# Turning attention probabilities with transposing DMAs instead of TensorE, in a mixture-of-experts and attention kernel

## The reference

```python
x = x + 0.5 * ffn(layernorm(x))      # 8 experts, 256 -> 512 -> 256, top-p weights, p = 0.9
x = x + attn(layernorm(x))
x = x + 0.5 * ffn(layernorm(x))

# attn: 16 query heads, 4 key/value heads of 16, rms norm and rotary on q and k
s = einsum('bhqd,bhkd->bhqk', q * scale, k)
s = where(causal, s, -inf)
p = softmax(s, axis=-1)              # 256 x 256 per head
out = einsum('bhqk,bhkd->bqhd', p, v) @ Wo.T + bo
```

## Time and profile before

| | |
|---|---|
| median of 3 runs | 1284.58 us (1283.86 to 1286.27) |
| profiled execution | 1287.02 us, its span 1285.2 us |
| TensorE matmul busy | 1203.9 us, 94% of the span |
| VectorE, ScalarE, GpSimd busy | 909.6, 574.2 and 543.9 us |
| mean granted TensorE clock | 0.989 of full |
| attention stages n = 12 to 27 | about 350 to 1030 us |

### The profile page before, as it was taken

One profiled execution on the slowest core, in us unless ns is written; L12 is line 12 of the kernel. 1 busy time (PEld: TensorE's weight loads), 2 busy tenths in 40 slices (PEclk: granted clock), 3 DMA queues, 4 the chain that ended last, 5 costly groups with the idle time before them and its releaser, 6 DMA issues.

```text
span 1285.2 us, 26968 instructions
## 1 busy us (share of the span) xinstructions
PE 1203.9 (94%) x8096; PEld 743.2 (58%) x8096; DVE 909.6 (71%) x1946; ACT 574.2 (45%) x1086; POOL 543.9 (42%) x659
## 2 busy tenths in 40 slices
PE   3777779999999999999999999999999999999999
PEld 2334435666566666655666666566665666665665
DVE  5767666567788887887788778878876755554444
ACT  2343343333364645554545454545554433333332
POOL 3324225355555455544554555445333333332332
PEclk9899989999999999999999999999999999999999
DMA  5122110000000000000000000000000000000000
GB/s 196 49 68 76 53 49 2 1 2 1 1 1 1 2 2 2 0 0 0 0 0 0 0 0 0 0 1 6 5 6 1 5 5 5 5 5 5 4 4 21
DMA packets 10048, 18.62 MB, mean 14 GB/s; under 512 B 2177, under 2 KB 6785, under 8 KB 9985
## 3 DMA queue, kind: packets, MB, share of 16 engines
q1 hardware_dynamic: 9840, 17.79, 4.1%
q10 hardware_dynamic: 144, 0.01, 0.0%
HBM read 15.70 MB, written 2.10 MB: 14 GB/s over the span
## 4 chain that ended last, share of the span: by engine, by line
PE 53%; issue 17%; DVE 15%; ACT 6%; POOL 5%; DVEq 2%; DMA 1%; ACTq 0%; POOLq 0%
PE U L212 15%; PE G L212 15%; PE YB L238 12%; PE BC L238 4%; ACT room L486 3%; POOL HS L882 2%; DVE X L584 2%; ACT TS L443 2%; DVE MX L713 2%; DVE TS L558 1%; DVE MXW L640 1%; DVE PR L619 1%; PE BB L381 1%; PE BC L357 1%; DVE NB L718 1%
## 5 line engine op out<-in xcount | busy, mean ns | idle before, releaser
L882 POOL TENSOR_TENSOR HS<-H,HS 128x512 f16<-128x512 f32 x256 | 299.0, 1169 | 469.8 <-ACT HS L450 420.7
L212 PE MATMUL G<-XS,W 128*128 128x512 f16 (+1 forms) x1536 | 382.0, 384 | 37.7 <-DVE H L565 23.3
L212 PE MATMUL U<-XS,W 128*128 128x512 f16 (+1 forms) x1536 | 380.0, 384 | 2.1 <-DVE W L660 1.6
L558 DVE SCALAR_TENSOR_TENSOR TS<-TS,G 128x512 f32<-128x512 f32 x256 | 175.4, 685 | 234.0 <-ACT TS L443 232.1
L238 PE MATMUL YB<-W,HS 128*128 (+1 forms) x2340 | 291.6, 274 | 28.3 <-DVE X L584 20.5
L450 ACT ACTIVATE HS<-H 128x512 f16<-128x512 f32 x256 | 162.9, 636 | 341.6 <-DVE H L565 337.2
L443 ACT ACTIVATE TS<-G,TSC 128x512 f32<-128x512 f32 x256 | 175.9, 687 | 251.5 <-PE U L212 250.5
L238 PEld LDWEIGHTS YB<-W,HS 128*128 128x128 f16 x2340 | 224.0, 98 | 95.7 <-DVE X L584 30.7
L212 PEld LDWEIGHTS U<-XS,W 128*128 (+1 forms) x1536 | 151.5, 99 | 190.1 <-issue 10.7
L212 PEld LDWEIGHTS G<-XS,W 128*128 (+1 forms) x1536 | 147.3, 100 | 172.0 <-issue 26.6
L565 DVE SCALAR_TENSOR_TENSOR H<-TS,U 128x512 f32<-128x512 f32 x256 | 175.8, 687 | 35.3 <-DVE TS L558 22.8
(11 more groups left out here) (174 smaller groups left out, 1221.6 us busy)
## 6 DMA issues: line engine op xcount, KB each, us to landing
room<-in_gate SPq DMA_DIRECT2D x7, 512.0 KB, 3.2
room<-in_up SPq DMA_DIRECT2D x7, 512.0 KB, 3.4
room<-in_down SPq DMA_DIRECT2D x7, 512.0 KB, 3.2
X<-in_x SPq DMA_DIRECT2D x4, 512.0 KB, 10.5
out_y<-X SPq DMA_DIRECT2D x16, 128.0 KB, 1.7
W<-in_gate SPq DMA_DIRECT2D x1, 512.0 KB, 7.7
W<-in_up SPq DMA_DIRECT2D x1, 512.0 KB, 8.2
W<-in_down SPq DMA_DIRECT2D x1, 512.0 KB, 8.9
```

Source lines behind the costliest of these rows:

```text
L212: mm = eng.matmul(bank[:, :], W[:, e, wl, j, k * I + m * P:k * I + (m + 1) * P], XS16[:, xpar(n), xl, k, :, :].rearrange('p a b -> p (a b) ...
L558: eng.scalar_tensor_tensor(TS[:, i % 2, :], TS[:, i % 2, :], 1.0, GB[i % 2][:, :], ALU.add, ALU.mult).then_inc(L['v_ff'].sem, 1)
L882: eng.tensor_tensor(HS[:, h, 1, m, :], H32[:, i % 2, :], HS[:, h, 0, m, :], ALU.subtract).then_inc(L['g_ff'].sem, 1)
```

## The change

P32 is no longer turned by TensorE. It is split where it lies, in the orientation in which the exponentials were written: `act_ph` copies P32 to PH, `dve_pl` makes PL = P32 - PH, and SP issues two transposing DMAs per item, PH to PHT and PL to PLT, each of twelve 128 x 128 blocks. PL takes the place of P32's first part, so `act_exps` of the next item waits for the DMA that reads PL, and each of the three `dve_pl` waits for the one ahead.

```diff
-        PH, PL = (room[:, NP3 + j * NP3 // 2:NP3 + (j + 1) * NP3 // 2].bitcast(F16)... for j in range(2))
+        PH = room[:, NP3:NP3 + NP3 // 2].bitcast(F16)...
+        PLT = room[:, NP3 + NP3 // 2:2 * NP3].bitcast(F16)...
+        PL = room[:, 0:NP3 // 2].bitcast(F16)...
+        PHT = sb('PHT', [P, 3, G, P], F16)
...
+        def turned(n, it):
+            return 16 * (2 * (n - 12) + it + 2)
...
-        def pe_pt(eng, n, act, it):
...
-                for g in range(G):
-                    mm = eng.transpose(bank[:, g * P:(g + 1) * P], P32[:, b, g, :], ident[:, :])
...
-        def pe_pv(eng, lane, m, ready, kv):
-            eng.wait_ge(*L['v_hd'].at(m, ready))
+        def pe_pv(eng, lane, m, it, kv):
+            eng.wait_ge(s_thi, turned(m, it))
+            eng.wait_ge(s_tlo, turned(m, it))
...
-                        for ph in (PH, PL):
+                        for ph in (PHT, PLT):
...
-                if p == 1 and 'pw' in act:
-                    pe_pv(eng, 'p_pw', n - 1, 'l1.2', 2 * ((n + 1) % 2) + 1)
+                if p == 6 and 'pw' in act:
+                    if 'hd' in act:
+                        eng.wait_ge(*L['a_hd'].at(n, 'e0.7'))
+                    else:
+                        eng.wait_ge(*L['v_hd'].at(n - 1, 'rd0'))
+                    pe_pv(eng, 'p_pw', n - 1, 1, 2 * ((n + 1) % 2) + 1)
...
-                if p == 6 and 'hd' in act:
-                    pe_pt(eng, n, act, 0)
...
-                if p == 9 and 'hd' in act:
-                    pe_pv(eng, 'p_hd', n, 'l0.2', 2 * (n % 2))
+                if p == 14 and 'hd' in act:
+                    eng.wait_ge(*L['a_hd'].at(n, 'e1.7'))
+                    pe_pv(eng, 'p_hd', n, 0, 2 * (n % 2))
...
         def act_exps(eng, n, it, qt, heads):
...
-            eng.wait_ge(*L['p_hd'].at(n if it else n - 1, 'pt0.2' if it else 'pt1.2'))
+            eng.wait_ge(s_tlo, turned(n, it - 1))
...
         def act_ph(eng, n, it):
-            eng.wait_ge(*L['p_hd' if it else 'p_pw'].at(n, 'pv0' if it else 'pv'))
-            for b, bank in enumerate((BA, BB, BC)):
-                eng.wait_ge(*L['p_hd'].at(n, f'pt{it}.{b}'))
-                eng.activation(PH[:, b, :, :]..., bank[:, :], ACT.Copy)
+            eng.wait_ge(s_thi, turned(n, it - 1))
+            for b in range(3):
+                if b == 1:
+                    eng.wait_ge(*L['a_hd'].at(n, f'e{it}.7'))
+                else:
+                    eng.wait_ge(*L['g_hd'].at(n, f'k{it}.{b // 2}'))
+                eng.activation(PH[:, b, :, :]..., P32[:, b, :, :]..., ACT.Copy)
...
         def dve_pl(eng, n, it, bs):
             for b in bs:
                 eng.wait_ge(*L['a_hd'].at(n, f'h{it}.{b}'))
-                eng.tensor_tensor(PL[:, b, :, :]..., (BA, BB, BC)[b][:, :], PH[:, b, :, :]..., ALU.subtract)
+                if b:
+                    eng.wait_ge(*L['v_hd'].at(n, f'l{it}.{b - 1}'))
+                eng.tensor_tensor(PL[:, b, :, :]..., P32[:, b, :, :]..., PH[:, b, :, :]..., ALU.subtract)
...
-                if p == 2 and 'pw' in act:
+                if p == 7 and 'pw' in act:
                     dve_sum(eng, n, 'v_pw', '', 'p_pw', 'pv')
...
+                if p == 15 and 'hd' in act:
+                    dve_sum(eng, n, 'v_hd', '0', 'p_hd', 'pv0')
+                    dve_ob(eng, n, 'v_hd', '0', n, 2 * (n % 2))
                 if p in (7, 15) and 'hd' in act:
                     dve_pl(eng, n, p // 8, (0, 1, 2))
...
-                if p == 10 and 'hd' in act:
-                    dve_sum(eng, n, 'v_hd', '0', 'p_hd', 'pv0')
...
-                    if p == 2 and 'pw' in act:
+                    if p == 8 and 'pw' in act:
                         dve_ob(eng, n, 'v_pw', '', n - 1, 2 * ((n + 1) % 2) + 1)
-                    if p == 10 and 'hd' in act:
-                        dve_ob(eng, n, 'v_hd', '0', n, 2 * (n % 2))
...
+            def turn(n, it):
+                eng.wait_ge(*L['a_hd'].at(n, f'h{it}.2'))
+                if it:
+                    eng.wait_ge(*L['p_hd'].at(n, 'pv0'))
+                else:
+                    eng.wait_ge(*L['p_pw'].at(n, 'pv'))
+                eng.dma_start_transpose(PHT..., PH...).then_inc(s_thi, 16)
+                eng.wait_ge(*L['v_hd'].at(n, f'l{it}.2'))
+                eng.dma_start_transpose(PLT..., PL...).then_inc(s_tlo, 16)
+
+            def sp_body(n, act):
+                if 'hd' in act:
+                    turn(n, 0)
+                if 'st' in act:
+                    store(n, n - 24)
+                if 'hd' in act:
+                    turn(n, 1)
```

More of the change, by code:

```diff
@@ L66, in build @@
         P32 = room[:, 0:NP3].rearrange('p (b g k) -> p b g k', b=3, g=G)
-        PH, PL = (room[:, NP3 + j * NP3 // 2:NP3 + (j + 1) * NP3 // 2].bitcast(F16).rearrange('p (b g k) -> p b g k', b=3, g=G) for j in range(2))
+        PH = room[:, NP3:NP3 + NP3 // 2].bitcast(F16).rearrange('p (b g k) -> p b g k', b=3, g=G)
+        PLT = room[:, NP3 + NP3 // 2:2 * NP3].bitcast(F16).rearrange('p (b g q) -> p b g q', b=3, g=G)
+        PL = room[:, 0:NP3 // 2].bitcast(F16).rearrange('p (b g k) -> p b g k', b=3, g=G)
+        PHT = sb('PHT', [P, 3, G, P], F16)
         early = W[:, E - 2, :, :, :].rearrange('p a j w -> p (a j w)').bitcast(F32).rearrange('p (j w) -> p j w', j=3)
@@ L153, in build @@
         s_st = sem('s_st')
+        s_thi, s_tlo = (sem('s_thi'), sem('s_tlo'))
         items = range(2)
         L = {}
[L156 removed]
@@ L254, in pe_qkv @@
         def pe_qkv(eng, n, act):
[L256 to L259, removed]
+            eng.wait_ge(*L['a_rt'].at(n - 1, 'ex'))
             eng.wait_ge(*L['a_ap'].at(n - 1, 'xt'))
@@ L363, in pe_op_tp @@
             if 'pw' in act:
-                eng.wait_ge(*L['v_hd'].at(n - 1, 'l1.1'))
-            else:
+                eng.wait_ge(*L['a_hd'].at(n - 1, 'e1.7'))
+            if 'op' in had(n, act):
                 eng.wait_ge(*L['v_op'].at(n - 1, 'ad'))
@@ L488, in act_ph @@
         def act_ph(eng, n, it):
[L489 to L492 removed]
+            eng.wait_ge(s_thi, turned(n, it - 1))
[4 more added lines that the diff above has]
+                    eng.wait_ge(*L['g_hd'].at(n, f'k{it}.{b // 2}'))
+                eng.activation(PH[:, b, :, :].rearrange('p a b -> p (a b)'), P32[:, b, :, :].rearrange('p a b -> p (a b)'), ACT.Copy).then_inc(L['a_hd'].sem, 1)
         def act_ap_xt(eng, n):
@@ L675, in dve_qn, with dve_rb @@
             eng.tensor_tensor(QN[:, :].rearrange('p (h c) -> p h c', c=HD), QKV[:, 0:QK * HD].rearrange('p (h c) -> p h c', c=HD), RR[:, :].unsqueeze(2).broadcast_to([P, QK, HD]), ALU.mult).then_inc(L['v_a3'].sem, 1)
-        def dve_rb(eng, n, a):
+        def dve_rb(eng, n, a, act):
+            if a == 0 and 'ap' in had(n, act):
+                eng.wait_ge(*L['p_ap'].at(n - 1, 'tp'))
             eng.wait_ge(*L['v_a3'].at(n, 'qn'))
@@ L980, in pool_body @@
                     pool_rs(eng, n, 'v_al', 'g_al', 'a')
-                if p == 4 and 'os' in act:
+                if p == 10 and 'os' in act:
                     pool_os(eng, n, act)
@@ L1044, in store @@
                 eng.dma_start(d['out'][t, :, :], X[:, t, :]).then_inc(s_st, 16)
-            for a, b in RUNS:
-                if 'st' in active(a):
-                    if b - a == 1:
-                        store(a, a - 24)
-                    else:
-                        with eng.Fori(a, b) as n:
-                            store(n, n - 24)
+            def turn(n, it):
[4 more added lines that the diff above has]
+                    eng.wait_ge(*L['p_pw'].at(n, 'pv'))
+                eng.dma_start_transpose(PHT[:, :, :, :].rearrange('p b g q -> p (b g) q'), PH.rearrange('p b g k -> p (b g k)')).then_inc(s_thi, 16)
+                eng.wait_ge(*L['v_hd'].at(n, f'l{it}.2'))
+                eng.dma_start_transpose(PLT[:, :, :, :].rearrange('p b g q -> p (b g) q'), PL.rearrange('p b g k -> p (b g k)')).then_inc(s_tlo, 16)
+            def sp_body(n, act):
[5 more added lines that the diff above has]
+                    turn(n, 1)
+            eng.sem_inc(s_thi, 16)
+            eng.sem_inc(s_tlo, 16)
+            for n in range(RANGES['hd'][0], RANGES['st'][1] + 1):
+                sp_body(n, active(n))
             for m in range(BT):
```

60 lines of the change are left out of this document (25 added, 35 removed).

## The result

The changed kernel takes 1330.24 us in the median of four runs (1328.65 to 1332.49), against 1285.42 us for the kernel before (four runs, 1283.86 to 1290.75). The ratio is 1.0342, with a 95% interval of 1.0308 to 1.0376: slower by 3.4%. The execution profiled after took 1330.08 us, its span is 1327.9 us.

A forecast was written before the change was run, and what follows sets the result against it. In nine full stages the chain runs mostly through VectorE and ScalarE, not TensorE. 2.5 us slower each (22.5) plus 10 for seven others gave 32.5, so 1317 us on the 1284.58 median; range 1274 to 1366.

The forecast's parts named there:

- What is removed: TensorE's transposes, 2.62 us per stage, 41.9 at most; truly got back only PV leaving slot 9, 0.61 us.
- Step 1: Slots 7 to 9, full stage: moved sum, waits, HS make X 1.9 us later, y4 1.2; less PV, 0.6 late.
- Step 3: Slot 15, full stage: sum, OB, waits and HS make X 2.5 us late; slot 2 without its sum minus 0.54; net 1.9.
- The other seven: Stages n = 12, 13, 14, 24 to 27: more room on VectorE; 1.3 to 1.5 us each with exclusion, 10 us.
- Late DMAs: Rival: transposing DMAs take 10.5 us each where 7.1 are free; 12.4 us a stage, some 1515 us; 13%.
- GpSimd's power operation: Rival: RR behind HS of slot 7 keeps the third PL out; y4 3.4 us later in thirteen stages, 1361 us; 8%.
- The faster case: Rival: VectorE hides its additions and TensorE sets the time; 1276 us, at the utmost 1243; 12%.
- the case without exclusion: Rival: PL and HS do not exclude each other, but waits and moved sums count; 1292 us, between 1288 and 1304; 12%.
- The signs: Profile after: PL over 1 us or gaps ended by HS; y4, y2 waiting longer; TensorE busy about 40 us less; DMAs 3 to 5 us.

The follow-up runs named there:

- The first two experiments: PL's first input from PSUM on the kernel after (PL then holds PH): 1310.64 us; both PL inputs in SBUF on the kernel before: 1308.67 us.
- 1284.48: Kernel after with PL's first input from PSUM (PL then holds PH) and item 0's sum and OB in slot 2 of the next stage: ratio 0.9974.
- 1310.64: Kernel after with PL's first input from a PSUM bank instead of P32 (PL then holds PH): ratio 1.0175.
- 1270.09: Kernel after with one PL per item, sums and OB in slots 2 and 10, WTC between TS and H in slots 8 and 14: ratio 0.9867.

## Why the prediction was right, and where it was off

The forecast was 1317.0 us in a range of 1274 to 1366, slower with 83%. It came out at 1330.24, 13 us over the forecast and just past the 1304 to 1330 that were given half the chance. The sign and the mechanism are as told. Of the 13 us, 6 are the nine full stages, 4 the seven others, and 2.5 the step down from the profiled execution to the median of before, which the kernel after did not show (1330.08 and 1330.24).

*What is removed.* "What TensorE truly gets back is PV leaving slot 9", 0.61: from y4's start to the scores of item 1, 781.64 to 785.57, 3.93 us pass instead of 4.50, so -0.57. y2 to y3 is 5.91 against 5.92, so the transposes that left slot 6 gave nothing, as worked out.

*Step 1, slots 7 to 9.* Forecast: `X` 1.9 late and y4 1.2. Measured: 1.84 and 1.29 (y3 to y4 6.89 instead of 5.60). That the 1.84 came so near is partly luck. The sum is 0.54 and HS held the PL for 0.84 (2.97 less 2.13), both as forecast, but the waits among the three PL cost 0.25 together and not 0.56, and 0.21 that the forecast did not have is `X` waiting for WTC.

*Step 3, slot 15.* Forecast 2.5 for `X` behind H; measured 4.70 instead of 2.40, so 2.3. HS held OB rather than the first PL, for 0.79 (0.9 forecast), and PL's waits cost 0.25 again; OB with the wait for its own sum took 0.7 rather than 0.48. Then the term that was mis-sized: "Slot 2 has lost its sum: minus 0.54". It gave nothing. From `X` of slot 15 to y2, 755.98 to 768.84, there are 12.86 us, and 12.87 before. RA's end was already set by HS: at 691.28 it ran 0.90 us behind the sum, and the time that the sum left was filled by RA's own waiting, 1.24. The rule of this kernel that I used for PL and OB I had not applied to RA, which is in the same rows. So the step is +2.45 (some 0.15 arises ahead of H of slot 15) and not 1.9. The sum for a full stage is 1.29 - 0.57 + 2.45 = 3.17 against 3.15 measured and 2.5 forecast: 5.9 us over nine stages.

*The other seven.* Forecast 1.3 to 1.5 each, 10 together; measured 14. n = 12 to 14 took 42.67, 43.18 and 43.64 us against 40.03, 40.38 and 40.83: 2.6 to 2.8 more. n = 24 came out at 1.45 (42.20 against 40.75). By the starts of their first H, n = 25 to 27 took 0.3, 2.8 and 1.2 more. I had counted on room on VectorE that in n = 12 to 14 is not there. With one input in PSUM those three take 40.91, 41.46 and 41.94, so 1.7 of the 2.7 is exclusion; with item 0's sum in slot 2 as well, 40.07, 40.66 and 41.12, so another 0.8 is the moved sum and OB, which the full stages pay too.

Of the 2.8 of n = 26, 1.7 is the clock, in this one trace:

```profile
982.00:984.00 2.00, 2.00 (x6) 0.63 (x5) 1.41 (x3) 0.63 (x1) 0.29 (x1) 0.50 0.25 47
```

From 982 to 985.2 us the granted clock is 0.50, the 1.2 GHz level, and six gate matmuls take 2.77 us instead of 1.46. TensorE had waited 1.80 us for an `X` update before 980.16. It waited as long at that place in the kernel without the transposing DMAs, whose clock stayed at 1.00 and whose n = 26 took 1.1 more than before. What set the fall off is open.

*The range and the rivals.* Late DMAs: fallen, by 3.6 us to land and by the kernel without them. By the Trainium skill, "Advanced Engine Details and Errata", section "X-Bar Transpose (TRN2)", they are as fast as regular DMAs; the trace agrees roughly, with the 3.2 us of a 512 KB load and 3.6 for these 384 KB. The 1309 ns that the Trainium skill, "VectorE: DVE Perf Modes", section "The three transpose paths", gives for one 128x128 block do not add up over blocks: twelve landed in 3.6.
GpSimd's power operation: fallen for PL. RR ran from 779.46 to 783.45, and the last PL ran beside it from 780.08 to 780.77, in its usual 0.69. The flat rule of the Trainium skill, "SBUF — State Buffer", section "SBUF: two separate sides", a lock for the full instruction, would have kept it out until 783.45.
The faster case and the case without exclusion needed PL and HS to pass each other. The first two experiments show that they do not when both inputs of PL lie in SBUF, and do when one lies in PSUM; with one in PSUM and item 0's sum in slot 2 the time is 0.26% under that of before, just past the 0.2% that I set for no change.

*The signs.* PL of over 1 us, y4 waiting (1.23 us) and DMAs landing in 3.6 came as told. y2 did not wait longer, 0.86 as before; the longer waits for `X` stood at y7 (1.38 instead of 0.44), y0 (0.72 instead of none) and y1 (0.40 instead of none). TensorE's busy time fell by 20.6 us and not by 40, half of what the distances between starts say. The y products show 7.7 us more than before, 299.3 instead of 291.6; the rest was not taken apart.

*What settled what.* That the exclusion of PL and HS is worth 20 us is shown from both sides (added to the kernel before, taken out of the one after). That the rest is the move of item 0's sum and OB is shown by 1284.48 against 1310.64, 26 us. Part of these is exclusion too, since in slot 15 of the full stages HS held OB; how much was not measured by itself. That the change itself (transposes off TensorE) can be had at a gain is shown by 1270.09.

## What to carry to other kernels

Where an operand of VectorE moves from PSUM to SBUF, look up which GpSimd operations run beside it: the price is not in its duration alone but in who waits, and it passes to the next instruction with two SBUF inputs, however small. Ask of every instruction near the removed one whether its end is set by its start or by the other engine; only in the first case does an earlier start give anything. TensorE's 97% busy said nothing on what taking work from it would give: that was read from the chain, 0.6 us a stage; and the removal paid only once what VectorE does beside GpSimd was rearranged.

## What the runs showed that was not expected

- The size of the instruction decides nothing about the wait: WTC, 0.15 us alone, took 0.72 to 1.12 us beside an HS, OB 1.07 instead of 0.28. Each ended with HS or within 0.15 us of it.
- The exclusion goes both ways and is settled at the start of an instruction: HS took 1.41 us behind a PL of 0.69 and 1.94 or 2.48 behind one of 1.75, each time ending 1.0 us behind it. Three short ones let GpSimd in between; one long one that starts first does not.
- The power operation RR grew from 3.55 to 3.99 us when it started beside a PL with two SBUF inputs, and stayed at 3.55 with one input in PSUM. It did not keep the next PL out.
- A wait of VectorE on its own instruction ahead cost 0.12 us between PL and PL; H behind TS idles 0.19.
- A transposing DMA of 384 KB landed in 3.6 us and took SP 1.44 us to issue. The packets on SP's queue went from 9840 to 110192 with them, and nearly all of the added ones are below 512 bytes (102528 in the whole trace against 2177). No effect on the engines was seen.
